# Four attention layers on one core: biases folded into additions on GpSimd, stack presets moved there, loads and gate spread cut in pieces, a new step order

## What is computed

```python
# layer 0 (phase 0)
x = x + attention @ Wo.T + bo
# layer 1 (phases 1, 2, MLP), gates g per batch and half of the tokens
x = x + g_msa * (mha(mod(ln(x))) @ attn_proj_w + attn_proj_b)
x = x + g_mca * (cross(mod(ln(x))) @ crs_proj_w + crs_proj_b)
x = x + g_mlp * (gelu(mod(ln(x)) @ fc1_w + fc1_b) @ fc2_w + fc2_b)
# layer 2 (phase 3)
x = ln(attention @ W_o.T + b_o + x) * gamma + beta
# layer 3 (phase 4)
x = x + (attention(ln(x), ctx) @ quant(Wo).T + bo)
```

## Time and profile before

| | us |
|---|---|
| median of three runs (316.63 to 322.85) | 316.98 |
| the profiled execution | 320.48 |
| its span, first to last instruction | 318.6 |
| TensorE busy | 279.7 |
| VectorE busy | 228.2 |
| ScalarE busy | 216.4 |
| GpSimd busy | 185.7 |

### The profile page before, as it was taken

The page is one execution under the profiler, slowest core; times in us unless marked ns, Lnnn a source line. Parts: engine busy times, 40 slices in busy tenths (PEclk is TensorE's granted clock), DMA queues, the critical chain, the costliest instruction groups (busy, mean ns, idle before and its releaser), DMA issues.

```text
span 318.6 us, 9133 instructions
## 1 busy us (share of the span) xinstructions
PE 279.7 (88%) x3268; PEld 173.6 (54%) x3268; DVE 228.2 (72%) x473; ACT 216.4 (68%) x462; POOL 185.7 (58%) x349
## 2 busy tenths in 40 slices
PE   2576688999979999988998999899999989999996
PEld 1462344465554666665676686657564546435535
DVE  4898859978872682776472687694979898888733
ACT  1023158668866768667788758898968786788972
POOL 3717414454764668787586759662879787851100
PEclk9977579999995999999999999999999999999999
DMA  4548911421382203333213212220123121220002
GB/s 132 149 110 254 289 24 35 110 59 37 92 245 67 72 26 80 99 84 83 71 45 84 52 52 54 52 69 10 44 61 77 37 67 44 72 74 23 3 3 66
DMA packets 40644, 24.75 MB, mean 78 GB/s; under 512 B 4880, under 2 KB 39576, under 8 KB 40344
## 3 DMA queue, kind: packets, MB, share of 16 engines
q1 hardware_dynamic: 37144, 17.71, 22.0%
q10 hardware_dynamic: 3072, 5.41, 5.2%
q0 software_dynamic: 384, 1.05, 1.1%
HBM read 7.56 MB, written 0.54 MB: 25 GB/s over the span
## 4 chain that ended last, share of the span: by engine, by line
PE 48%; DVE 12%; SPq 10%; DMA 10%; POOL 7%; issue 6%; ACT 5%; ACTq 1%; POOLq 0%; DVEq 0%
PE ps L705 9%; SPq L483 9%; PE ps L663 8%; PE ps L662 8%; PE ps L633 6%; DVE neg_max L978 5%; DMA q_stack<-max_rows_split 4%; PE ps L731 3%; PE ps L698 3%; PE ps L789 3%; DMA q_stack<-q_parts 2%; PE ps L800 2%; DVE k_stack L946 2%; PE ps L819 2%; ACT probs L844 2%
## 5 line engine op out<-in xcount | busy, mean ns | idle before, releaser
L978 DVE TENSOR_REDUCE neg_max<-ps 128x2 f32<-128x512 f32 (+1 forms) x256 | 160.0, 682 | 36.3 <-PE ps L662 35.8
L844 ACT ACTIVATE probs<-ps 128x512 f32<-128x512 f32 x256 | 134.4, 605 | 29.2 <-PE ps L663 26.8
L662 PE MATMUL ps<-k_stack,q_stack 62*128 62x256 bf16 (+1 forms) x640 | 62.9, 259 | 9.8 <-DMA q_stack<-q_parts 5.9
L663 PE MATMUL ps<-q_stack,k_stack 64*128 64x256 bf16 (+1 forms) x640 | 58.8, 254 | 10.2 <-DMA q_stack<-max_rows_split 5.9
L705 PE MATMUL ps<-probs,v_cols 128*32 128x256 f32 x768 | 55.3, 394 | 0.3 <-ACT probs L844 0.2
L662 PEld LDWEIGHTS ps<-k_stack,q_stack 62*128 62x128 bf16 x640 | 28.9, 96 | 39.6 <-issue 10.3
L663 PEld LDWEIGHTS ps<-q_stack,k_stack 64*128 64x128 bf16 x640 | 29.4, 95 | 32.6 <-DMA q_stack<-max_rows_split 8.8
L705 PEld LDWEIGHTS ps<-probs,v_cols 128*32 128x32 f32 x768 | 20.4, 110 | 17.6 <-issue 8.8
L507 POOL CAST max_parts<-neg_max 128x16 bf16<-128x16 f32 (+2 forms) x34 | 6.8, 200 | 39.2 <-DVE neg_max L978 38.7
L876 ACT ACTIVATE q_f<-ps,vec 128x256 f32<-128x256 f32 x32 | 15.0, 476 | 8.2 <-PE ps L731 8.0
L894 ACT ACTIVATE heads_raw<-ps 128x512 f32<-128x512 f32 x20 | 12.0, 600 | 12.6 <-PE ps L705 7.8
(11 more groups left out here) (123 smaller groups left out, 451.5 us busy)
## 6 DMA issues: line engine op xcount, KB each, us to landing
k_stack<-k_parts SPq DMA_DIRECT2D x120, 64.0 KB, 2.1
q_stack<-q_parts SPq DMA_DIRECT2D x114, 64.0 KB, 2.1
gates<-gates_dram ACTq DMA_DIRECT2D x1, 1536.0 KB, 7.1
w<-in_w ACTq DMA_DIRECT2D x1, 1024.0 KB, 9.7
rows<-in_rows ACTq DMA_DIRECT2D x1, 704.0 KB, 6.0
q_stack<-max_rows_split SPq DMA_DIRECT2D x44, 4.0 KB
w<-in_w ACTq DMA_DIRECT2D x1, 576.0 KB, 7.1
ctx_t<-in_ctx_t SPq DMA_DIRECT2D x4, 128.0 KB, 2.9
```

The costliest lines, as they stand in the source:

```text
L662: return nc.tensor.matmul(out, queries, keys, start=True, stop=True)
L663: return nc.tensor.matmul(out, keys, queries, start=True, stop=True)
L844: nc.scalar.activation(probs[:, n % PROB_BUFS, :], ps[bank_of["score", p, b, i]][:, :], ACT.Exp, scale=SCALE).then_inc(of(st), 1)
L978: nc.vector.tensor_reduce(dst, src, AX.X, ALU.max, negate=True).then_inc(of(st), 1)
```

## The change

- `out_proj` and `fc2` no longer write a bias. A new step `base` (stream "b", GpSimd, five per batch) adds the bias row, or gate times bias, to x ahead of time into a new tile `base`, and `add_out` adds that instead of x and waits for it. `base_mlp` (stream "B", one per batch) does the same for the MLP.
- `gate_fold` now also multiplies the bias rows by the gates (in place in `gates`), and has a third form for the MLP's bias: 12 steps with 20 instructions instead of 8 with 8. `gated_bias` and its two instructions on VectorE are gone.
- The presets of the stacks go from VectorE to GpSimd, as 32-bit words. Batch 0's preset and `clear_v` now come ahead of the first gather there.
- The weight group of 1024 KB is cut in three (phase 1, phase 2, MLP). Two loads still come ahead of most max steps (x, then `rows`), the other five later. The spread of the gates is one DMA per batch, each with its own semaphore.
- `ORDER`, `BANK_OF` and `COUPLED` are new throughout.
- The diff also writes an `apply` on ScalarE and a `deviation` step, and a form of `take_k`/`take_q` that writes the first part too; with `APPLY_ON` all "pool" and `PART_ON` "act" for phase 0 alone, none of them is used.

```diff
 MAX_T_ON = ("act", "act", "act", "act", "dve")
+PART_ON = ("act", "pool", "pool", "pool", "pool")
 APPLY_ON = ("pool", "pool", "pool", "pool")
+LOADS = ("x", "rows", 2, 1, 3, 4, 5)
+SPREADS = B
+W_GROUP = (0, 1, 3, 5, 5)
...
-        "Y": ("dve", only([("preset", 0, 0)], not first)),
+        "Y": ("pool", only([("preset", 0, 0)], not first)),
...
+        "b": ("pool", [("base", p, 0) for p in phases]),
+        "B": ("pool", [("base_mlp", 2, 0)]),
+        "Z": ("pool", [("gate_fold", i, 0) for i in range(3)]),
...
 ORDER = (
-    "Y2Y1K0R0z0r0Q0r0K1I1R1z1D0D0k0Q1q0I210R2z2r1y0E0r100I300E000y0W01010D1D1k19090Q2W190K2r2d2r2J1y190M0M0M0m0m0W2q1"
...
+    "I1Q0K0I2R0z0Q1r0D0k010K1R1z1R2r0D0y0q000r1r1D1k110J1E000y010Q2Y1E000D1y1y1z211K290I3r2r2Y2M0M0m0M0M0M0M01111q1j1"
...
-W_GROUPS = (("v0", "o0"), ("q1", "fc2d"), ("ada0", "ada8"), ("q3", "o4"))
+W_GROUPS = (("v0", "o0"), ("q1", "o1"), ("ada0", "ada8"), ("q2", "o2"), ("fc1a", "fc2d"), ("q3", "o4"))
...
+        def preset_stacks(ops, b):
+            ops.memset(q_stack[:, b, :, :].rearrange("p e t -> p (e t)").bitcast(F32), 0.0)
+            return ops.memset(k_stack[:, b, :, :].rearrange("p e t -> p (e t)").bitcast(F32), TWO_ONES)
...
             nc.gpsimd.memset(mean_mat[:, :], 1.0 / (D * D)).then_inc(mean_set, 1)
+            clear_v(FIRST[1]).then_inc(first_v_cleared, 1)
+            preset_stacks(nc.gpsimd, FIRST[1]).then_inc(first_preset, 1)
             pool.wait_ge(pos_ready, 1)
             gather(FIRST[1])
-            clear_v(FIRST[1]).then_inc(first_v_cleared, 1)
...
+                    if p < 2:
+                        pool.wait_ge(w_loaded[W_GROUP[p + 1]], 16)
+                        pool.wait_ge(*done("rope", 0, b, 0))
+                        link(nc.gpsimd.tensor_tensor(rope_gated_o[:, 2 * b:2 * b + 2, p, :],
+                                                     w[:, W_AT[f"o{p + 1}"]:W_AT[f"o{p + 1}"] + 1, :].broadcast_to([P, NT, D]),
+                                                     gates[:, 2 * b:2 * b + 2, p, :], ALU.mult))
+                        g = gates[:, 2 * b:2 * b + 2, p, :]
+                        nc.gpsimd.tensor_tensor(g, g, row2(f"bo{p + 1}"), ALU.mult).then_inc(of(st), 1)
+                    else:
+                        nc.gpsimd.tensor_tensor(gate_bias[:, 2 * b:2 * b + 2, :], gates[:, 2 * b:2 * b + 2, 2, :],
+                                                row2("bfc2"), ALU.mult).then_inc(of(st), 1)
+                elif kind == "base":
...
+                    add = gates[:, 2 * b:2 * b + 2, p - 1, :] if p in (1, 2) else row2({0: "bo0", 3: "bo3", 4: "bo4"}[p])
+                    nc.gpsimd.tensor_tensor(base[:, b, :, :], x[:, b, :, :], add, ALU.add).then_inc(of(st), 1)
...
                 elif kind == "out_proj":
-                    pe.wait_ge(const_loaded, 16)
-                    pe.wait_ge(rows_loaded, 16)
-                    if p in (1, 2):
-                        pe.wait_ge(*done("take_gate", 0, 0, 0))
-                    for qt in range(NT):
-                        nc.tensor.matmul(out[:, qt * D:(qt + 1) * D], *bias_rows(b, qt, p), start=(qt == 0), stop=False,
-                                         skip_group_check=True)
...
-                                                start=False, stop=(qt == NT - 1), skip_group_check=True)
+                                                start=True, stop=True)
...
                     for qt in range(NT):
-                        nc.tensor.matmul(out[:, qt * D:(qt + 1) * D], ident[:, 0:1].broadcast_to([P, P]),
-                                         rows[:, R_AT["bfc2"], :], start=True, stop=False)
...
+                    n = 2 * 3 * D
+                    act.dma_start(gates[:, 2 * i:2 * i + 2, :, :].rearrange("p r k c -> p (r k c)"),
+                                  gates_dram[n * i:n * (i + 1)].partition_broadcast(P)).then_inc(gates_spread[i], 16)
...
                     dve.wait_ge(*done("out_proj", p, b, 0))
...
+                    dve.wait_ge(*done("base", p, b, 0))
...
-                                            x[:, b, :, :], ALU.add).then_inc(of(st), 1)
+                                            base[:, b, :, :], ALU.add).then_inc(of(st), 1)
```

More of the change, by code:

```diff
@@ L96, in streams @@
         "x": ("dve", [("stats", p, i) for p in phases[:-1] for i in range(1 + (p == 3))]),
-        "p": ("dve", [("apply", p, 1) for p in phases[:-1] if APPLY_ON[p] == "dve"]),
+        "p": ("pool", [("deviation", p, 1) for p in phases[:-1] if APPLY_ON[p] == "act"]),
         "f": ("dve", [("add_mlp", 2, 0)]),
@@ L127, in streams @@
         "3": ("sp", [("stack_max", p, g) for p, g in groups]),
-        "4": ("act", only([("spread", 0, 0), ("spread", 0, 1)], first)),
-        "9": ("act", only([("load", 0, i) for i in range(5)], first)),
+        "4": ("act", only([("keep_gates", 0, 0)] + [("spread", 0, i) for i in range(SPREADS)], first)),
+        "9": ("act", only([("load", 0, i) for i in range(len(LOADS))], first)),
         "5": ("sp", [("store", PHASES - 1, 0)]),
@@ L142 @@
[L142 to L146, removed]
@@ L234, in signal @@
             return own[kind]
-        if kind in ("stack_k", "stack_q", "gather", "load", "spread"):
+        if kind in ("stack_k", "stack_q", "gather", "load", "keep_gates", "spread"):
             return None
@@ L278, in build @@
         last_of_bank[bank] = st
-    chunks = [st for st in steps if st[0] == "exp"]
-    chunk_no = {st: n for n, st in enumerate(chunks)}
     mlps = [st for st in steps if st[0] == "add_mlp"]
@@ L287, in mlp_no @@
         return mlps.index(("add_mlp", 2, b, 0)) + 1
+    chunks = [st for st in steps if st[0] == "exp"]
+    chunk_no = {st: n for n, st in enumerate(chunks)}
     def value_of(chunk):
@@ L372, in build @@
         gates_stored = sem("gates_stored")
-        gates_spread = sem("gates_spread")
+        gates_spread = [sem(f"gates_spread{i}") for i in range(B)]
         out_stored = sem("out_stored")
@@ L589, in _ @@
                     gather(b)
+                elif kind == "preset":
+                    preset_stacks(nc.gpsimd, b).then_inc(of(st), 1)
                 elif kind == "clear_v":
@@ L620, in _ @@
                 elif kind == "apply" and i == 0:
-                    inverse_deviation(p, b, 0)
+                    pool.wait_ge(*done("base", p, b, 0))
+                    link(inverse_deviation(p, b, 0))
                     link(apply_norm(nc.gpsimd, b, heads_t_gated))
@@ L854, in _ @@
                 elif kind == "load":
-                    load_w(act, (2, 1, 3)[i - 2])
-                elif kind == "spread" and i == 0:
+                    load_w(act, LOADS[i])
+                elif kind == "keep_gates":
                     act.wait_ge(*done("take_gate", 0, 0, 0))
@@ L930, in _ @@
                     last.then_inc(of(st), 1)
+                elif kind == "apply":
+                    act.wait_ge(*done("deviation", p, b, 1))
+                    src = (heads_t_gated if p == 1 else x)[:, b, :, :]
+                    for qt in range(NT):
+                        last = nc.scalar.activation(heads_normed[:, b, qt, :], src[:, qt, :], ACT.Identity,
+                                                    bias=shift[:, b, qt:qt + 1], scale=rstd[:, b, qt:qt + 1])
+                    last.then_inc(of(st), 1)
                 elif kind == "take_x_t":
@@ L1036, in _ @@
                     dve.wait_ge(*done("fc2", p, b, 0))
-                    dve.wait_ge(gates_spread, 16)
+                    dve.wait_ge(*done("base_mlp", p, b, 0))
+                    dve.wait_ge(gates_spread[b], 16)
                     product = heads_normed[:, b, :, :]
```

215 lines of the change are left out of this document (120 added, 95 removed).

## The result

The changed kernel takes 299.75 us in the median of four runs (298.25 to 303.17), against 319.15 us for the kernel before in the runs of the same comparison (the median of 316.98 us shown ahead of the prediction was of the first three of them). The ratio is 0.940, with a 95% interval of 0.926 to 0.954; a later comparison gave 0.944 (0.931 to 0.957). Ratios are taken from the faster executions of each kernel alone, since some executions of any of these kernels take over 1.5% longer than its fastest, while medians and lists of runs have them all.

What follows compares the result with a forecast made beforehand. Bound: a start set by VectorE, gathers and DMA engines, then a long middle mostly by TensorE. Sum -6.2 - 5.8 - 3.2 + 1.0 + 3.1 - 0.5 = -11.6 us, from 316.98 to 305.4 us; range 297 to 315.

Steps and rivals of the forecast that it cites:

- 1, the bias groups: Bias matmuls L789, L816 on TensorE: 24 groups of 0.44 us leave the stream; -6.2 us, bounds 0 and 10.6.
- of the other 8.8 I take half: Bias groups before the last 8 us: half of their 8.8 us counted as on the path; the tail's 1.8 counted fully.
- The filler theory: TensorE's bias groups only fill gaps, so removal becomes idle time; with the start refilled -4.5, 312.5 us, chance 0.25.
- 2, the presets: Memsets leave VectorE: first rotation 4.3 us earlier, fourth preset 1.5; -5.8 us, bounds 0 and 7.3.
- The cover on GpSimd: GpSimd before the first gather: memsets end at 4.4, row indices ready at about 4.8, leaving 0.4 us of cover.
- The lock: Port pair shared by VectorE and GpSimd: position steps wait for a running memset, up to 1 us; left out of the sum.
- 4.3 us put down to the presets: VectorE's first rotation (L995) could start at 11.97 instead of 16.30 without the memsets: -4.3 us for everything behind it.
- what may be late next are the gathers for the other batches: Start, after earlier rotations: other batches' gathers may be late; new order puts batch 1's behind batch 0's; no separate size.
- 3, loads: Weight loads and gate spreads, cut and later: half of 6.4 us of transfer waits, -3.2; extra issues on ScalarE, +1.
- 4, GpSimd: 36 added GpSimd instructions, 26.2 us, 12% of it on the path: +3.1 us, bounds 0 and 26.2.
- The rival in which GpSimd becomes the bound between 100 and 200 us: Most of GpSimd's 36 added instructions stand ahead of deviations, normalisations, casts or splits: 325 us, slower; chance 0.10.
- 5, the order: All steps in new places, 185 couplings instead of 177, no row prices it: 0, with 5 us either way.

Runs made afterwards that it cites:

- the kernel at 0.989: Old order from the first max step on, start of the new order, all three edits, against the kernel before: ratio 0.989 (0.984 to 0.993).
- the one at 0.931: Changed kernel without biases of the output projections and second MLP layer, no base step or gate-bias product, against the kernel before: 0.931 (0.926 to 0.936).

## Why the prediction was right, and where it was not

**Direction and range: right; size too small by 7 us.** The actual saving of 18 to 19 us is 1.6 times the 11.6 of the sum. That the time fell inside the range was in part luck: the sum prices three edits and puts the order at 0, and the same three edits in the old order save nothing (1.0025).

**1, the bias groups.** The distance of 0.44 us per group was a good measure of what leaves TensorE: the undone groups cost 0.28 to 0.49 us each in the new order. The step that is in doubt is "of the other 8.8 I take half". The term was 6.2 us and came out at 6.6 to 11.7 in the new order, by the medians or by the ratios, so between half and all was on the path. In the old order the ratio gives 6.8 us, of which up to 1.3 are the earlier `clear_v`: there half was about right. The chain of the kernel before was misread here. It charges a group mostly with its whole duration, not with its distance to the next:

```profile
60.12 0.64 PE ps L789 x4
```

Its 8.3 us of L789 (2.6% of 318.6) are ten such groups of 0.64 to 0.71 us and the four at the end of 0.45, so 14 of the 20, not all; of L816 it has none. The filler theory (TensorE's idle time goes up by what its busy time loses) falls for the changed kernel with the 16.7 against 16.4 us from 100 us on; in the old order it holds in good part (21.2 and more).

**2, the presets.** The start went as worked out: rotation at 12.26 for a forecast 11.97, first max at 22.62 for 22. The cover on GpSimd was there and larger than the forecast 0.4 us: its memsets ended at 4.16, ahead of the row indices at 5.01. The lock is there: the position cast that began at 3.79 beside a memset of GpSimd took 0.40 us, its neighbours 0.17, and the row indices were ready at 5.01 instead of 4.79. In the kernel before, the same cast had no memset beside it and took 0.17:

```profile
3.81 0.17 DVE L950 CAST pos_f<-pos_i 128x8 f32<-128x8 int32 x1 [3.81 <-DMA pos_i<-in_pos]
```

By the rule in the Trainium skill, page "SBUF — State Buffer", section "Who interferes with whom", a wait until the end of that memset was to be expected, and 3.21 + 0.95 = 4.16 against 3.79 + 0.40 = 4.19 agrees. In the second profiled execution, where the cast began at 4.13, it took 0.17. The lock cost 0.2 us. It had cost more in the kernel before: L958 took 1.47 us and ended at 9.39, right behind GpSimd's `clear_v` memset (8.38 + 0.97 = 9.35), and in the old order with `clear_v` moved ahead the same operation, beside a gather alone, took 0.11. These 1.4 us in front of the rotations are a gain of moving `clear_v`; in the prediction they are among the 4.3 us put down to the presets. The size of the whole term was off: 10 to 12 us undone in the new order, 0.5 gained in the old order, where I had 5.8. I priced the presets by the first gap I saw, and not by what stands behind each of them in VectorE's queue up to the first scores. And "what may be late next are the gathers for the other batches" was named, but not followed into ScalarE's queue, where it decided.

**3, loads.** -3.2 and +1.0 were forecast; undone they cost 3.0 to 4.7 us. The small transfers in the chain became shorter but more: 3.87 us at 41.73, where a weight load was issued at 41.75, and 2.85 and 2.14 us beside a spread of 384 KB each, where the earlier trace rows has 4.83 and 5.11. Their share of the chain is 4% in both pages, 6% with the loads early. The shortest of the three:

```profile
73.50 2.14 DMA q_stack<-max_rows_split
```

Whether it was the cutting or the later place that did it was not tried.

**4, GpSimd.** +3.1 was forecast. The ratios give 4 us in the new order and the medians 1, so the term is not refuted and not confirmed. No wait of VectorE for a base shows in the profile after; the one wait around the bases is GpSimd's own, 0.7 us for add_out ahead of base_mlp. The rival in which GpSimd becomes the bound between 100 and 200 us did not come: it is busy for 84.6 of these 100 us (90 were worked out), and the stretch is no longer than before.

**5, the order.** "I take 0, with 5 us either way" is the step that failed most. Alone it is indeed worth 1 us (0.997). But an edit's price is not a number of its own: the presets are worth 0.5 us in the old order and 10 to 12 in the new, the biases at most 1.6 and 5.6 to 7.5. In the old order all three together give nothing. In the new one they give 17 us together (0.997 - 0.944), and undone one by one 18.7 by the medians or 24.6 by the ratios, so there they roughly add up. Which property of the new order behind the start makes the room is not settled. SyncE's issuing of transfers, 10% of the chain before and 3% after, is an obvious candidate, but it has only 4% in the kernel at 0.989 and 7% in the one at 0.931. What is shown is that the old order gives no room.

## What to carry to other kernels

Where each engine has its program in a fixed order, moving or removing work gives time only if the steps behind it may move up too: follow the step that comes free into the next queue, and ask what stands ahead of its consumer there. Price removed work on the bound engine by the distance from start to start (0.44 us here, not the 0.7 us of its busy sum). Count the groups that the chain holds instead of dividing its time by a distance: it held 14 of the 24, and the old order gave back about half of the 10.6 us that left TensorE. Compare where TensorE's idle time goes, and profile a kernel twice before reading a difference of a few microseconds at its start: the clock alone moved the first score by 2.6 us. To judge such a change, try both crosses, the old order with the new work and the new order with the old work; one cross alone (0.997) would have credited the edits with everything.

## What was not expected of the hardware

Busy time is not work. The same 3172 records of TensorE were busy for 272.4 us in the old order with the edits and for 258.8 in the changed kernel. The granted clock was 0.946 and 0.977 in these two executions. The second profiled execution of the changed kernel, at 0.949, separates the two parts:

```profile
PE 263.6 (87%) x3172; PEld 165.5 (55%) x3172; DVE 215.8 (72%) x463; ACT 215.1 (71%) x462; POOL 218.9 (73%) x393
```

So 4.8 us go between two executions of one kernel, with the clock, and 8.8 us lie between two orders at nearly the same clock. The busy time counts overlapping records once (the 96 bias records of the earlier trace rows have 16.8 us at some 290 ns each, 28 us in all), so the likely reason is that the new order has more of them overlap; that was not measured by itself.

At the start the clock follows the stops: from 20 to 40 us it was granted at 0.83 in the kernel after, whose TensorE waited 4.31 us once, and at 0.58 in the kernel with the presets on VectorE, where TensorE worked 12.63 of these 20 us:

```profile
20.00:40.00 20.00, 12.63 (x59) 7.80 (x58) 17.97 (x31) 4.04 (x12) 8.02 (x16) 0.58 0.46 117
```

It does not follow them alone: the second execution of the kernel after had nearly the same stops (3.62 us at that place) and was granted 0.66.
